# A three-block transformer layer on one core: work by token halves around the latent attention, latents from residual rows, and four-quarter rotary scores

## The chip, the core and the metric

The kernel runs on one core of a Trainium2 chip. TensorE (PE) multiplies matrices into PSUM, VectorE (DVE), ScalarE (ACT) and GpSimd (POOL) work on rows, SyncE (SP) issues nearly all transfers. The metric is the device time in microseconds of one execution. Before the change three runs took 791.65, 786.32 and 791.51 us, median 791.51.

## The reference

There are 256 tokens of 512 values, x, and 4096 context tokens. Three blocks follow each other, each on a layer-normed x, and each is added to x:

```python
x = x + xattn(layernorm(x), ctx, mask, ...)   # 16 heads of 32 over 4096 keys, then an output norm, times gamma, plus beta
x = x + attn(layernorm(x), ...)               # latent attention, causal, 16 heads, below
x = x + ffn(layernorm(x), ...)                # router, top 8 of 48 kept experts, 192 hidden values each
# latent attention
cq = rms_norm(h @ w_qa.T, q_a_ln_w)           # 384 latents; q = cq @ w_qb.T: per head 128 plain + 64 rotary
ckv = h @ w_kva.T                             # 128 latents + 64 rotary key values that all heads share
k_nope, v = split(rms_norm(ckv[..., :128], kv_a_ln_w) @ w_kvb.T)   # per head 128 + 128
pe = pe * cos + rotate_half(pe) * sin         # for queries and for the shared key
out = softmax(causal(q @ k.T * scale)) @ v; return out @ w_o.T
# experts
logits = x @ gate_weight.T; probs = softmax(masked logits); top 8, renormalised
each expert takes its first 192 tokens; y = (silu(x @ g.T) * (x @ u.T)) @ down.T; weighted sum over a token's experts
```

## The kernel before

Everything is written by hand, engine by engine: each engine runs its own list of instructions, and semaphores (`s["..."]`) tie them together. There is no scheduler. Where float16 is used, every operand is split in a high part (a cast on ACT) and a low part (the rest, on DVE), and a product is three matmuls. 256 tokens are two tiles (halves) of 128.

**Cross attention** (to about 336 us) goes over eight context blocks; the change leaves it as it is but for its last output products and one helper, `prep_experts`, that DVE ran in the last block.

**First way around** (L781 to L815 on DVE, L1143 to L1161 on PE). DVE adds the bias to each half's product `d_ps`, takes mean and variance, scales, adds x (this is `x1_sb`), takes mean and variance again and writes the normed rows `xn`. POOL computes each inverse root. PE turns `xn` (transposes), ACT copies the turned rows to `xT`, PE multiplies by `wlatT` to the latents (384 + 128 columns) and to the rotary keys, once as they are and once with their two halves swapped (columns written twice in the weights). Root mean squares, scaling, turning (`lat_ps`), and the split into `lath` and `latl` follow. Then the first pair's projections, in the order q, rotary q (with swapped copies), k, v.

**Eight pairs of heads** (`mla_pair` on each engine). On PE: scores of pair m (plain part, then rotary part, for each half), projections of pair m+1 (q, rotary q plain and swapped, k), output product of pair m-1 for half 0, turning of the probabilities, output product for half 1, the product with v, projection of v. On DVE: causal mask, row maxima, probabilities' scaling, low parts, rotation of the queries (five operations), low part of the output weights, low part of pair m+2's q weights (`split_q`, L699), low part of the result. PE waits for DVE at `p_ready` and for ACT at `pt_ready`.

**Second way around** (L891 on): the sum into `x1_sb`, the norm of both halves, turning, logits, top 8, counts over earlier tokens (`tri`, `ones`), router weights `ex`, turned to `wT`, gathered by the one-hot `emap` to 48 rows `wnew`, stored to memory (`w_scratch`) and loaded back as rows repeated over 64 partitions (`wb`).

**72 expert units** of 128 hidden values. On PE `gate_up(n)` is 24 matmuls of 256 columns, `down(n)` six of 512; the order is gate_up(0), gate_up(1), down(0), gate_up(2), down(1) and so on. ACT takes the silu, DVE multiplies (L930), weighs with `wb` (L933) and splits into `hh`, `hl`. Each unit's weights (768 KB) are loaded and split, ACT `uwh` (L557), DVE `uwl` (L875). The splits of units 0, 1 and 2 stand on DVE before pair 6, before pair 7 and after pair 7.

PE's matmuls all pass through one helper, L962, so its lines don't tell them apart; tiles and shapes do.

## Time and profile before

| | us |
|---|---|
| median of three runs | 791.51 |
| the profiled execution's own time | 791.05 |
| its span, first to last instruction | 789.3 |
| PE busy | 741.8 (94%) |
| DVE busy | 607.5 (77%) |
| ACT busy | 410.9 (52%) |
| mean granted TensorE clock | 0.978 |

In a row of instruction groups stand the line, engine, operation, tiles, shapes and count, then total busy us and the mean ns of one, then the idle time before. In a timeline row the first number is the start in us from the span's start, the second the duration of the row's instructions together; in brackets stands how long the engine had been idle and who released it. A PE row's duration includes the drain of its last matmul, in which the next row has already begun. A stretch row gives the stretch, its length, and for each engine busy us and instructions; then the granted TensorE clock (1.00 is 2.4 GHz, 0.50 is 1.2 GHz), the DMA engines' busy share and GB/s. The chain of waits gives PE 71% of the span, 19% to issue on an engine that waited for nothing shown, 5% to DVE, 2% to ACT.

### The profile page before, as it was taken

The numbers are of one execution on the slowest core, as the hardware profiler recorded it, in microseconds if no ns is written. First come the engines' busy times: TensorE is split into PE (matmuls) and PEld (weight loads), VectorE is DVE, ScalarE is ACT, GpSimd is POOL, SyncE is SP. The second block draws the span as 40 slices with busy tenths as digits, with TensorE's granted clock in tenths as the row PEclk, the third lists the DMA queues.
The fourth block names the chain that finished last, engine by engine and source line by source line (L and its number), as shares of the span: only waits on it lengthen the run. The fifth ranks groups of instructions, "written<-read, shape, count | busy, mean of one in ns | idle before, by whom it ended". The sixth has DMA issues, their size and how long they took to land.

```text
span 789.3 us, 16744 instructions
## 1 busy us (share of the span) xinstructions
PE 741.8 (94%) x6813; PEld 458.9 (58%) x6813; DVE 607.5 (77%) x964; ACT 410.9 (52%) x538; POOL 10.3 (1%) x29
## 2 busy tenths in 40 slices
PE   8999999999999998977999966699999999999997
PEld 3544444444444444435777744477777777777774
DVE  4598888888888887745798855488888888888885
ACT  3666676666667676403567642244444444444441
POOL 2000000000000000010000000000000000000000
PEclk9999999999999999989999987999999999999999
DMA  8910110101000100050242200397777777776760
GB/s 321 336 56 15 42 53 3 56 2 55 2 2 1 55 2 3 1 213 0 81 152 88 105 1 0 107 285 237 235 234 233 233 233 233 233 238 229 238 230 27
DMA packets 30211, 96.09 MB, mean 122 GB/s; under 512 B 6048, under 2 KB 15696, under 8 KB 27728
## 3 DMA queue, kind: packets, MB, share of 16 engines
q1 hardware_dynamic: 29872, 95.33, 36.4%
q8 instruction: 39, 0.64, 0.3%
q14 instruction: 12, 0.10, 0.0%
q10 hardware_dynamic: 288, 0.02, 0.0%
HBM read 94.73 MB, written 0.57 MB: 121 GB/s over the span
## 4 chain that ended last, share of the span: by engine, by line
PE 71%; issue 19%; DVE 5%; ACT 2%; DMA 1%; POOL 0%; POOLq 0%; DVEq 0%; SPq 0%; ACTq 0%
PE pS L962 31%; PE pP L962 24%; PE pD L962 8%; PE pO L962 8%; DVE xT L740 2%; ACT arena L467 2%; DVE arena L629 0%; PE pS L974 0%; DVE bn L776 0%; DMA arena<-w_scratch 0%; DMA w_scratch<-arena 0%; DVE xn L623 0%; DVE arena L755 0%; PE pS L1146 0%; DVE x_sb L789 0%
## 5 line engine op out<-in xcount | busy, mean ns | idle before, releaser
L962 PE MATMUL pS<-arena 128*128 128x256 f16 (+1 forms) x2178 | 260.4, 277 | 4.6 <-DVE arena L814 1.9
L962 PEld LDWEIGHTS pS<-arena 128*128 128x128 f16 (+1 forms) x2178 | 217.8, 102 | 51.8 <-issue 6.9
L962 PE MATMUL pP<-arena 128*128 128x512 f16 x968 | 237.1, 384 | 2.5 <-DVE arena L629 2.5
L962 PEld LDWEIGHTS pP<-arena 128*128 128x128 f16 x968 | 91.2, 99 | 127.9 <-issue 24.3
L467 ACT ACTIVATE arena<-pS,mblk 128x1024 f32<-128x1024 f32 x128 | 147.3, 1201 | 14.1 <-PE pS L962 11.5
L875 DVE SCALAR_TENSOR_TENSOR arena<-arena 128x1536 f16<-128x1536 f32 x72 | 126.1, 1752 | 3.0 <-ACT arena L557 3.0
L728 DVE TENSOR_SCALAR arena<-arena 128x1024 f32<-128x1024 f32 x128 | 88.3, 692 | 43.3 <-ACT arena L467 40.0
L574 ACT ACTIVATE arena<-pS 128x256 f32<-128x256 f32 x72 | 27.7, 384 | 164.2 <-PE pS L962 164.2
L557 ACT ACTIVATE arena<-arena 128x1536 f16<-128x1536 f32 x72 | 106.3, 1477 | 0.8 <-DMA arena<-in_units 0.8
L962 PE MATMUL pO<-arena 128*32 128x256 f32 (+6 forms) x1272 | 100.1, 366 | 2.7 <-DVE arena L835 2.7
L962 PE MATMUL pD<-arena 128*128 128x512 f16 x288 | 77.2, 382 | 7.5 <-DVE arena L937 6.0
L962 PEld LDWEIGHTS pO<-arena 128*32 128x32 f32 (+3 forms) x1272 | 43.3, 107 | 38.1 <-issue 18.0
L930 DVE TENSOR_TENSOR arena<-pS,arena 128x256 f32<-128x256 f32 x72 | 30.6, 424 | 38.7 <-ACT arena L574 38.7
L962 PE MATMUL pS<-work,arena 32*128 32x256 f16 x1536 | 53.4, 269 | 3.2 <-ACT arena L467 3.0
L962 PEld LDWEIGHTS pS<-work,arena 32*128 32x128 f16 x1536 | 33.9, 93 | 32.5 <-issue 24.5
L409 ACT ACTIVATE arena<-pP,xb 128x512 f32<-128x512 f32 x29 | 20.0, 688 | 46.2 <-PE pP L962 46.2
L962 PEld LDWEIGHTS pD<-arena 128*128 128x128 f16 x288 | 27.9, 98 | 25.6 <-DVE arena L937 6.7
L933 DVE TENSOR_TENSOR arena<-arena 128x256 f32<-128x256 f32 x72 | 30.7, 426 | 13.1 <-DMA arena<-w_scratch 5.7
L740 DVE TENSOR_TENSOR xT<-xT,arena 128x1024 f32<-128x1024 f32 x28 | 34.2, 1222 | 1.5
L740 DVE TENSOR_TENSOR arena<-arena 128x1024 f32<-128x1024 f32 x28 | 34.2, 1222 | 1.5
L414 ACT ACTIVATE arena<-pP 128x512 f32<-128x512 f32 x29 | 17.3, 597 | 31.6 <-PE pP L962 31.6
L937 DVE TENSOR_TENSOR arena<-arena 128x256 f16<-128x256 f32 x72 | 30.7, 426 | 2.5
(191 smaller groups left out, 505.7 us busy)
## 6 DMA issues: line engine op xcount, KB each, us to landing
arena<-in_units SPq DMA_DIRECT2D x72, 768.0 KB, 4.8
arena<-w_scratch SPq DMA_DIRECT2D x144, 64.0 KB, 2.7
mw_in<-in_mla_in SPq DMA_DIRECT2D x8, 1024.0 KB, 7.7
...
```

The costliest lines, as they stand in the source:

```text
L409: act.activation(kf[:, n % 2], bank, ACT.Identity, bias=xb[:, 1, n:n + 1], scale=1.0 / SW).then_inc(s["proj_evac"], 1)
L414: act.activation(v_sb[:, p, n - HC], bank, ACT.Copy, scale=1.0 / (SA * SW)).then_inc(s["proj_evac"], 1)
L467: act.activation(probs[:, tile], step_scores(st), ACT.Exp, bias=mblk[:, p, 1, tile:tile + 1], scale=mblk[:, p, 0, tile:tile + 1])\
L557: act.activation(uwh[:, slot], uw32[:, slot], ACT.Copy, scale=SW).then_inc(s["unit_hi"], 1)
L574: act.activation(sg[:, buf], pS[:, bank, 0:T], ACT.Silu, scale=1.0 / (SA * SW)).then_inc(s["silu_ready"], 1)
L728: dve.tensor_scalar(probs[:, t], probs[:, t], LO, HI, ALU.max, ALU.min).then_inc(s["clip_done"], 1)
L740: dve.tensor_tensor(acc, acc, probs[:, t], ALU.add).then_inc(s["sum_done"], 1)
L875: dve.scalar_tensor_tensor(uwl[:, slot], uw32[:, slot], SW, uwh[:, slot], ALU.mult, ALU.subtract).then_inc(s["unit_lo"], 1)
L930: dve.tensor_tensor(m1[:, buf], pS[:, bank, T:2 * T], sg[:, buf], ALU.mult).then_inc(s["m1_ready"], 1)
L933: dve.tensor_tensor(m2[:, buf], m1[:, buf], wb[:, slot], ALU.mult).then_inc(s["m2_ready"], 1)
L937: dve.tensor_tensor(hl[:, buf], m2[:, buf], hh[:, buf], ALU.subtract).then_inc(s["h_lo"], 1)
L962: return pe.matmul(o, lhsT, rhs, start=start, stop=stop, **kw)
```

## The change

- **First way around.** The latents come from the turned residual rows `x1_sb` themselves. PE sums the columns of `wlatT` (`col_sums`), and DVE forms mean times column sum minus product (`center`), which is minus the centred latents; the inverse root of the layer norm isn't applied to the latents at all, their root mean square takes it in through a scaled epsilon (`epsv`). Only the rotary keys are scaled by it. Rotary keys are computed as rows (128 columns: plain and swapped), scaled, and turned. The halves go through one after the other; the cross attention's last products too. Twenty warming matmuls are gone. `prep_experts` moves behind the second statistics, and also clears the gate's unwanted columns.
- **Rotary scores.** A query's rotary part is projected once, without a swapped copy. It is multiplied by cosine and by sine (`qcs`, one operation), and the keys have two turned forms, so that the scores take two rotary products instead of one. The weights `mw_in` are 1152 instead of 1536 columns wide for q.
- **Pairs.** v's projection moves ahead of the turning; the first pair's order is k, v, rotary q, q; units 0, 1, 2 are split within pairs 4, 5, 6 (behind the maxima on DVE).
- **Last pair.** `mla_last_pair` goes by halves, with own banks and semaphores.
- **Second way around.** Norm, turning, logits and choice by halves; masking by a matmul of `nkeep` into the logits' bank; softmax's sum over the top 8 alone. The router weights of units 0 to 3 are spread over the partitions by PE itself (`bc_ps`), three units' gate_up stand before the first down, `wnew` is copied by ACT and stored later.
- **Experts.** Three `hh`/`hl` buffers, four `sg`, the first twelve units written out. Units 4 to 7 are loaded ahead, ahead of the store.

```diff
+            for n in range(RING):
+                sp.wait_ge(s["unit_lo"], n + 1)
+                load_unit(n + RING, n)
             sp.wait_ge(s["wn_ready"], 1)
             sp.dma_start(wdram, wnew[0:KEPT, :]).then_inc(s["w_stored"], 16)
             sp.wait_ge(s["w_stored"], 16)
-            for u in range(RING):
+            for u in range(RING, 2 * RING):
...
+                if proj:
+                    rope_hi(m + 1, 1 - p)
...
+                dve.scalar_tensor_tensor(x1_sb[:, t, :], work[:, t, :], rstd[:, t:t + 1], x_sb[:, t, :],
+                                         ALU.mult, ALU.add).then_inc(s["xn_ready"], 1)
+            for t in range(TT):
+                dve.wait_ge(s["xn_ready"], t + 2)
                 half_stats(x1_sb, t)
+                dve.tensor_scalar(epsv[:, t:t + 1], mv[:, t, 1:2], 1e-5, 1e-6, ALU.add, ALU.mult)
                 dve.tensor_scalar(var[:, t:t + 1], mv[:, t, 1:2], 1e-5, None, ALU.add).then_inc(s["var_ready"], 1)
-            for t in range(TT):
+            prep_experts()
...
+                dve.scalar_tensor_tensor(latc[:, t], colsum[:, 0:LAT], mv[:, t, 0:1], pS[:, 2 + t, :],
+                                         ALU.mult, ALU.subtract).then_inc(s["latc_ready"], 1)
...
-                dve.wait_ge(s["lrstd_ready"], t + 1)
-                dve.tensor_scalar(cqn[:, t], pS[:, 2 + t, 0:QLR], lrs[:, t, 0:1], None, ALU.mult)
-                dve.tensor_scalar(kvn[:, t], pS[:, 2 + t, QLR:QLR + KVLR], lrs[:, t, 1:2], None, ALU.mult)\
...
-                dve.scalar_tensor_tensor(rp1, pS[:, 1, 0:T], SH / (SA * SW), cosT[:, :], ALU.mult, ALU.mult).then_inc(s["rope_step"], 1)
-                dve.scalar_tensor_tensor(rp2, pS[:, 1, T:2 * T], SH / (SA * SW), sinT[:, :], ALU.mult, ALU.mult).then_inc(s["rope_step"], 1)
...
-                dve.tensor_tensor(qpel[:, p], rp1, qpeh[:, p], ALU.subtract).then_inc(s["rope_ready"], 1)
...
+            center(0)
+            scale_kpe(0)
+            add_eps(0)
+            norm_latents(0)
+            center(1)
+            scale_kpe(1)
+            add_eps(1)
+            norm_latents(1)
...
+                dve.scalar_tensor_tensor(qcs, pS[:, 1, 0:T].unsqueeze(1).broadcast_to([128, 2, T]), SH / (SA * SW), cs,
+                                         ALU.mult, ALU.mult).then_inc(s["rope_mul"], 1)
...
+                dve.tensor_tensor(qpel[:, p], qcs, qpeh[:, p], ALU.subtract).then_inc(s["rope_ready"], 1)
...
+                dve.scalar_tensor_tensor(qcs, kpeT, SH, cs[:, 0].unsqueeze(1).broadcast_to([128, 2, T]), ALU.mult, ALU.mult)
...
+                if unit is not None:
+                    split_unit(unit, unit)
...
+                    rope_mul(m + 1, 1 - p)
                     lo_q(m + 1, 1 - p)
-                    rope_q(m + 1, 1 - p)
                     lo_k(m + 1, 1 - p)
+                    rope_lo(m + 1, 1 - p)
...
+            rope_k_products()
+            lo_latents()
+            rope_k()
+            lo_k(0, 0, 1)
+            rope_mul(0, 0, 3)
...
+                for t, (lo, hi) in enumerate(((0, 128), (128, 384))):
+                    dve.wait_ge(s["exps_done"], m + 1 + t)
+                    dve.reciprocal(rc[:, t], sm[:, t]).then_inc(s["rec_ready"], 1)
+                    dve.wait_ge(s["rec_ready"], m + 1 + t)
+                    for j in range(2):
+                        last = dve.tensor_scalar(pm[:, j, lo:hi], pm[:, j, lo:hi], rc[:, t, j:j + 1], None, ALU.mult)
+                    last.then_inc(s["p_ready"], 1)
...
+            for t, o in enumerate((pD, pP)):
+                dve.wait_ge(s["mla_done"], t + 1)
+                link(dve.scalar_tensor_tensor(x1_sb[:, t, :], o[:, :], 1.0 / (SH * SW), x1_sb[:, t, :], ALU.mult, ALU.add))
+                half_stats(x1_sb, t)
+                dve.tensor_scalar(var[:, t:t + 1], mv[:, t, 1:2], 1e-5, None, ALU.add).then_inc(s["var_ready"], 1)
...
-            for t in range(TT):
+            for t in range(TT):
+                pe.wait_ge(s["ctxn_ready"], 2)
                 out_rows(t, (2,))
-            for t in range(TT):
                 pe.wait_ge(s["ctxn_ready"], t + 3)
                 out_rows(t, (3,)).then_inc(s["delta_done"], 1)
...
-            keep_warm(20)
-            pe.wait_ge(s["lat_in"], 16)
...
+            def col_sums(o, lo, hi):
+
+                for c in range(HC):
+                    last = mm(o, ones[:, :], wlatT[:, c, lo:hi], c == 0, c == HC - 1)
+                last.then_inc(s["col_mm"], 1)
...
-                    last = pe.transpose(pS[:, t, 128 * c:128 * c + 128], xn[:, t, 128 * c:128 * c + 128], ident[:, :])
+                    last = pe.transpose(pS[:, t, 128 * c:128 * c + 128], x1_sb[:, t, 128 * c:128 * c + 128], ident[:, :])
...
+            def rotary_keys(t):
                 for c in range(HC):
-                    at = QLR + KVLR + 128 * r
-                    last = mm(pO[:, 1, T * r:T * r + T], wlatT[:, c, at:at + 128], xT[:, c, :], c == 0, c == HC - 1)
-            last.then_inc(s["kpe_mm"], 1)
-            for t in range(TT):
+                    last = mm(kpe_ps[t], xT[:, c, 128 * t:128 * t + 128], wlatT[:, c, LAT:], c == 0, c == HC - 1)
...
+            pe.wait_ge(s["lat_in"], 16)
+            col_sums(pD[:, :], 0, LAT)
+            turn_rows(0)
+            pe.wait_ge(s["ctxn_ready"], TT + 2)
+            col_sums(pO[:, 1, 0:2 * DR], LAT, LAT + 2 * DR)
+            turn_rows(1)
+            latents(0)
+            rotary_keys(0)
+            latents(1)
+            rotary_keys(1)
+            pe.wait_ge(s["col_ready"], 2)
+            turn_keys(0)
+            turn_latents(0)
+            turn_keys(1).then_inc(s["kpe_tr"], 1)
+            turn_latents(1).then_inc(s["lat_tr"], 1)
...
-                for r in range(2):
+                for r in ((1, 0) if first else (0, 1)):
...
-                    for j in range(2):
+                    for j in range(2 - r):
...
-                        for j in range(2):
-                            last = mm(pO[:, j, lo:hi], q[64 * j:64 * j + 64, p, 128 * t:128 * t + 128],
-                                      w[64 * j:64 * j + 64, 0:hi - lo], False, k == 2)
-                last.then_inc(s["s_done"], 1)
+                        for i in range(2):
+                            for j in range(2):
+                                r = slice(64 * j, 64 * j + 64)
+                                last = mm(out_of(t, j, lo, hi), q[r, p, i, 128 * t:128 * t + 128], w[r, i, 0:hi - lo],
+                                          start and k == 0 and i == 0, stop and k == 2 and i == 1)
...
+                nope(0, 0, 128, True, False)
+                half = rotary(0, 0, 128, False, True)
+                if apart:
+                    half.then_inc(s["s_done"], 1)
+                    pe.wait_ge(s["qkv_ready"], 3 * m + 3)
+                rotary(1, 128, 384, True, False)
+                nope(1, 128, 384, False, True).then_inc(s["s_done"], 1)
...
                     out_product(m - 1, 1 - p, 0)
+                pe.wait_ge(s["qkv_ready"], 3 * m + 3)
+                if proj:
+                    proj_v()
...
-                pe.wait_ge(s["qkv_ready"], 3 * m + 3)
                 if proj:
-                    pe.wait_ge(s["rope_step"], 4 * m + 6)
+                    pe.wait_ge(s["rope_mul"], m + 2)
...
-                if proj:
-                    proj_v()
...
+            proj_k(0, first=True)
+            proj_v()
             proj_q(0, first=True)
-            pe.wait_ge(s["lat_lo"], QC + 1)
-            proj_k(0)
...
+            def mla_last_pair(m, p):
+
+                def turned(t):
+                    pe.wait_ge(s["p_ready"], m + 1 + t)
+                    for j in range(2):
+                        for i in range(t + 1):
+                            at = 128 * (t + i)
+                            last = pe.transpose(tail_s[t][:, j, 128 * i:128 * i + 128], pm[:, j, at:at + 128], ident[:, :])
+                    last.then_inc(s["pt_done"], 1)
+
+                def weighted(t):
+                    pe.wait_ge(s["pt_ready"], m + 1 + t)
+                    for j in range(2):
+                        for i in range(t + 1):
+                            last = mm(tail_o[t][:, j, :], vv[:, p, i, 128 * j:128 * j + 128],
+                                      pt[:, j, 128 * (t + i):128 * (t + i) + 128], i == 0, i == t)
+                    last.then_inc(s["o_done"], 1)
+
+                mla_scores(m, p, apart=True)
+                out_product(m - 1, 1 - p, 0)
+                turned(0)
+                weighted(0)
+                turned(1)
+                out_product(m - 1, 1 - p, 1)
+                weighted(1)
+                for t in range(TT):
+                    out_product(m, p, t, last=True).then_inc(s["mla_done"], 1)
+
...
+            keep_warm(8, pS[:, 0, :])
...
+                pe.wait_ge(s["xT_ready"], t + 4)
+                mm(pO[:, t, 0:NEXP], ident[:, :], nkeep, True, False)
+                for c in range(HC):
+                    last = mm(pO[:, t, 0:NEXP], xT[:, c, 128 * t:128 * t + 128], gateT[:, c, :], False, c == HC - 1)
+                last.then_inc(s["logits_done"], 1)
...
+            gate_up(1, 1, 1)
             pe.wait_ge(s["w_ready"], 1)
...
-            mm(pS[0:KEPT, 3, 0:T], emap, wT, True, True).then_inc(s["wn_done"], 1)
+            for n in range(RING):
+                e = 2 * (n // 3) + (0 if n % 3 == 2 else n % 3)
+                pick = pick2 if n % 3 == 2 else emap[:, e:e + 1].broadcast_to([128, 128])
+                last = mm(bc_ps[:, n], pick, wT, True, True)
+            last.then_inc(s["bc_done"], 1)
+            mm(wn_ps, emap, wT, True, True).then_inc(s["wn_done"], 1)
+            gate_up(2, 2, 2)
...
+                    if not (last_turn and u + 1 >= UNROLL) and not (first and u < 2):
                         gate_up(n + 1, (u + 1) % 3, (u + 1) % RING)
```

PE in one pair of the loop, before: 24 matmuls of scores, then 42 of projections (`pS`, 128x256).

```order
L962 MATMUL pO<-arena 128x128 x12
L962 MATMUL pO<-arena 128x256 x12
L1170 REGISTER_ALU
L1171 REGISTER_ALU
L1173 REGISTER_ALU
L962 MATMUL pS<-arena 128x256 x42
L962 MATMUL pD<-arena 128x512 x6
L1237 MATMUL pO<-ident,arena 128x128 x6
L962 MATMUL pP<-arena 128x512 x6
```

And with the change:

```order
L1113 MATMUL pO<-arena 128x128 x18
L1113 MATMUL pO<-arena 128x256 x18
L1348 REGISTER_ALU
L1349 REGISTER_ALU
L1351 REGISTER_ALU
L1113 MATMUL pS<-arena 128x256 x33
L1113 MATMUL pD<-arena 128x512 x6
L1435 REGISTER_ALU
L1113 MATMUL pS<-arena 128x256 x6
L1441 MATMUL pO<-ident,arena 128x128 x6
L1113 MATMUL pP<-arena 128x512 x6
```

Scores are 36 matmuls, 12 more, all rotary; the projections ahead of the output product fell from 42 to 33, and the six of v stand before the turning (`pO<-ident`) instead of at the pair's end.

PE from the last pair's scores to the sum of its output products, before:

```order
L962 MATMUL pO<-arena 128x128 x12
L962 MATMUL pO<-arena 128x256 x12
L962 MATMUL pD<-arena 128x512 x6
L1237 MATMUL pO<-ident,arena 128x128 x6
L962 MATMUL pP<-arena 128x512 x6
L962 MATMUL pS<-arena 128x256
L962 MATMUL pS<-arena 128x128
L962 MATMUL pS<-arena 128x256
L962 MATMUL pS<-arena 128x128
L962 MATMUL pD<-arena 128x512 x6
L962 MATMUL pP<-arena 128x512 x6
L962 MATMUL pD<-zero 128x512
```

And with the change:

```order
L1113 MATMUL pO<-arena 128x128 x18
L1113 MATMUL pS<-arena 128x256 x18
L1113 MATMUL pD<-arena 128x512 x6
L1469 MATMUL pO<-ident,arena 128x128 x2
L1113 MATMUL pS<-arena 128x128 x2
L1469 MATMUL pS<-ident,arena 128x128 x4
L1113 MATMUL pP<-arena 128x512 x6
L1113 MATMUL pS<-arena 128x128 x4
L1113 MATMUL pD<-arena 128x512 x6
L1113 MATMUL pP<-arena 128x512 x6
L1113 MATMUL pS<-zero 128x512 x8
```

The last pair's turning (`<-ident`) and its v products (`pS`, 128x128) are two halves, the second half's turning ahead of pair 6's second output product. The closing zero product (`pD<-zero`) is gone, and eight warming ones (`pS<-zero`) stand at the end.

PE around the router weights, from the counts to the first down products, before:

```order
L962 MATMUL pO<-arena,tri 128x128
L962 MATMUL pO<-arena,ones 128x128
L962 MATMUL pO<-arena,tri 128x128
L1308 MATMUL pS<-ident,arena 128x128 x2
L962 MATMUL pS<-arena 48x256
L1320 UNCONDITIONAL_BRANCH
L1320 ISA
L962 MATMUL pS<-arena 128x256 x24
L1291 REGISTER_ALU
L962 MATMUL pD<-arena 128x512 x3
L962 MATMUL pP<-arena 128x512 x3
```

And with the change:

```order
L1113 MATMUL pS<-arena,tri 128x128
L1113 MATMUL pS<-arena,ones 128x128
L1113 MATMUL pS<-arena,tri 128x128
L1113 MATMUL pS<-arena 128x256 x24
L1541 MATMUL pS<-ident,arena 128x128 x2
L1113 MATMUL pO<-arena 128x256 x4
L1113 MATMUL pS<-arena 48x256
L1113 MATMUL pS<-arena 128x256 x24
L1113 MATMUL pD<-arena 128x512 x3
L1113 MATMUL pP<-arena 128x512 x3
L1113 MATMUL pD<-arena 128x512 x3
L1113 MATMUL pP<-arena 128x512 x3
```

Four products with a picked column (`pO<-arena 128x256 x4`) are new, and three gate_ups (x24) stand before the first down (pD, pP) instead of two.

## Rows read from the trace of the kernel before

**Rows 1.** Stages: engines' busy us, granted TensorE clock, DMA.

```profile
0.00:335.90 335.90, 327.29 (x3759) 155.37 (x3760) 267.24 (x367) 216.44 (x245) 4.86 (x22) 1.00 0.17 59
335.90:373.80 37.90, 27.64 (x120) 16.41 (x119) 19.25 (x43) 7.91 (x19) 4.73 (x6) 0.86 0.28 111
373.80:477.00 103.20, 93.57 (x738) 68.66 (x738) 79.69 (x161) 59.60 (x124) 0.00 (x0) 0.95 0.23 82
477.00:504.90 27.90, 14.24 (x84) 11.33 (x84) 13.53 (x40) 6.54 (x12) 0.69 (x1) 0.81 0.05 14
504.90:785.00 280.10, 279.02 (x2114) 207.18 (x2114) 226.52 (x354) 120.43 (x138) 0.00 (x0) 0.99 0.70 224
```

**Rows 2.** Short stretches of TensorE alone: busy us, instructions, granted clock.

```profile
344.40:351.20 6.80, 5.80 (x10) 0.50 0.50 208
...
363.50:371.20 7.70, 7.55 (x50) 0.78 0.00 0
...
463.80:470.80 7.00, 3.72 (x12) 0.51 0.00 0
```

**Rows 3.** Instruction groups, 373 to 460 us: busy, mean ns, idle before.

```profile
L699 DVE SCALAR_TENSOR_TENSOR arena<-mw_in,arena 128x1536 f16<-128x1536 f32 x7 | 12.3, 1753 | 0.2 <-ACT arena L442 0.2
...
L830 DVE SCALAR_TENSOR_TENSOR arena<-pS,arena 128x512 f16<-128x512 f32 x7 | 4.8, 684 | 0.0
...
L529 ACT ACTIVATE arena<-pS 128x512 f16<-128x512 f32 x7 | 4.2, 597 | 4.4 <-PE pS L962 4.4
```

**Rows 4.** Timeline between the two attentions: start, us, instruction, idle before.

```profile
344.72 1.09 PE L1146 MATMUL pS<-ident,xn 128*128 128x128 f32 x4 [4.30 <-DVE xn L795]
...
346.49 6.02 PE L962 MATMUL pS<-wlatT,xT 128*128 128x512 f32 x8 [0.69 <-ACT xT L496]
...
353.64 3.70 PE L962 MATMUL pS<-wlatT,xT 128*128 128x512 f32 x8 [0.69 <-ACT xT L496]
...
361.70 0.84 ACT L550 ACTIVATE arena<-pS,lnw 128x256 f16<-128x256 f32 x2 [3.49 <-PE pD L1161]
...
373.79 2.38 PE L962 MATMUL pO<-arena 128*128 128x128 f16 x24 [2.67 <-DVE arena L835]
```

**Rows 5.** Timeline of one pair, and the next pair's start.

```profile
386.42 0.50 PE L962 MATMUL pO<-arena 128*128 128x128 f16 x6
...
387.88 0.50 PE L962 MATMUL pO<-arena 64*128 64x256 f16 x6
...
388.32 4.76 PE L962 MATMUL pS<-arena 128*128 128x256 f16 x42
...
392.45 1.01 DVE L859 TENSOR_SCALAR arena<-arena 128x128 f32<-128x128 f32 x4
...
398.17 1.97 PE L962 MATMUL pO<-arena 128*128 128x128 f16 x24
```

**Rows 6.** Timeline: pair 6's scores, then the last pair.

```profile
445.14 1.97 PE L962 MATMUL pO<-arena 128*128 128x128 f16 x24
...
458.12 1.97 PE L962 MATMUL pO<-arena 128*128 128x128 f16 x24
...
460.32 1.76 DVE L875 SCALAR_TENSOR_TENSOR arena<-arena 128x1536 f16<-128x1536 f32 x1 [1.34 <-ACT arena L557]
...
467.08 1.54 PE L1237 MATMUL pO<-ident,arena 128*128 128x128 f32 x6 [5.59 <-DVE arena L859]
```

**Rows 7.** Timeline, attention's sum to the first down product.

```profile
477.02 0.69 DVE L891 SCALAR_TENSOR_TENSOR x_sb<-pD,x_sb 128x512 f32<-128x512 f32 x1 [0.93 <-PE pP L962]
...
482.39 1.97 PE L974 MATMUL pS<-ident,xn 128*128 128x128 f32 x8 [5.41 <-DVE xn L623]
...
497.69 0.36 SPq L310 DMA_DIRECT2D w_scratch<-arena  x1
...
504.93 1.46 PE L962 MATMUL pD<-arena 128*128 128x512 f16 x3 [5.00 <-DVE arena L937]
```

**Rows 8.** Ten expert units, all engines.

```profile
512.00:551.15 39.15, 39.15 (x303) 29.34 (x301) 32.38 (x51) 17.69 (x21) 0.00 (x0) 1.00 0.80 257
```

487 lines of the change are left out of this document (296 added, 191 removed).

## The prediction

> **What bounds the kernel now.** I read the stages first [rows 1]. TensorE (PE) is busy 327.3 of 335.9 us in cross attention and 279.0 of 280.1 us in the expert units: both are full, and the change touches neither's inside. Between them stand 37.9 us of which PE works 27.6, partly at a low clock (0.86), 103.2 us of pairs of heads (93.6 busy, 0.95) and 27.9 us of which 14.2 are busy (0.81). What can be won lies in these 169 us. In the expert units ten take 39.15 us, 3.915 each, PE 100% busy, DVE 32.4 [rows 8]: work that is done before the first down product is no longer due behind it. Next the single waits. PE waits 4.30 us for the normed rows, 2.67 for the first pair's low parts [rows 4], 5.59 for the last pair's probabilities [rows 6], 5.41 for the normed rows of the second way around and 5.00 for the router weights' round trip through memory [rows 7]. Last the clock: after a stretch in which PE did little it is granted 0.50 (1.2 GHz): 344.4 to 351.2, about half of 363.5 to 371.2, 463.8 to 470.8 [rows 2]. The latents' first half took 6.02 us so, the second half 3.70 [rows 4].
>
> Prices [rows 3]: DVE 0.68 us for 512 columns, 1.75 for 1536 (in proportion between); ACT 0.60 for 512. A float32 product of 512 columns is 0.43 per MATMUL row (eight rows in 3.70 with a drain of about 0.3). A float16 one of 256 columns is 0.11 (42 in 4.76) [rows 5].
>
> **First way around.** Marks are those of the profiled execution. Half 0's bias sum can start 0.85 us sooner, because its last product no longer stands behind half 1's (two MATMUL rows of 0.43). PE turned `xn` at 344.72; it now turns `x1_sb`, written before the second statistics: those, the power on POOL and the scaling fall out, some 4.3 us, so PE turns half 0 at about 339.6. The column sums (3.4 and 0.9 us) run while PE would wait, in place of warming products, so they cost nothing and keep the clock up; if their cover went they would cost 4.3. Half 1 is turned at 341.1. Then PE is continuous: latents 3.4, keys 0.9, latents 3.4, keys 0.9, from 341.6 to 350.1. `prep_experts` (about 2.3 us of DVE) ends near 345.8, and half 0's latents are ready at 345.2: 0.6 late, hidden since DVE then waits for half 1. Half 1's latents are there at 349.5; centring 0.7, keys 0.8, squares on ACT 1.0, epsilon and power 1.0, scaling 0.6 end at 353.2, turning at 353.8, against 361.70: 7.9 us won. From there the scores came 12.1 us later. Now DVE is the chain: the keys' two products 1.3 (from 353.2), low parts of the latents 1.6, keys' sums and split 2.0, k 0.7, the query's rotation 0.7, its cast on ACT 0.7 and low part 0.7, q 0.7: 361.7. PE has 39 products (4.3 us at full clock) instead of 48 and is hidden behind this, unless it runs at 1.2 GHz: it idles most of 350 to 354, and then q's evacuation comes after 362.7 and the scores at 364. I take 363.3 for 373.79: **10.5 us won** (8 to 12).
>
> **Pairs 0 to 6.** A pair takes 11.75 us (386.42 to 398.17) and PE is never idle in it [rows 5]. q's projections lose nine products of 256: 9 x 0.11 = 0.98. The scores gain twelve rotary products. Do these cost what others cost? Six rotary ones of 256 columns start at 387.88 and the next block at 388.32 [rows 5]: 0.44 for six, where one behind another they take 0.66. So the two heads' products, on rows 0 to 63 and 64 to 127, run as pairs, and 0.44 is three pairs of 0.11 and about 0.1 of changing over. Added are three narrow and three wide pairs, 0.17 + 0.33 = 0.5. By the Trainium skill (TensorEngine Tiling (Array Packing), Key Properties) a change of the tiling mode drains TensorE; the trace agrees with its 0.1 per change. Both halves' rotary blocks now stand side by side, two changes instead of four: 0.2 less. Net 0.98 - 0.5 + 0.2 = 0.68 less, 11.1 a pair. v's projection is moved, not added. DVE follows if its chain is shorter: it was idle 0.2 us before a pair's mask, so 11.55; five rotary operations (1.9) become two of 512 (1.3), the low part of q's weights goes from 1536 to 1152 columns (-0.4): 10.5. The probabilities are scaled at 393.46, 5.1 us after the scores (388.4) [rows 5]; PE's wait for them stays covered: 33 products, the output product and v make 3.6 + 1.3 + 0.65 = 5.55. ACT's new cast (0.6) stands before its copy of the turned probabilities, which then ends at about 7.45 where PE asks at 7.5: covered by nothing to spare; without cover it costs 0.6 a pair. Pair 0, without output products, is a chain and not full: 11.4 instead of 12.6. Pairs 1 to 3 win 0.65 each. In pairs 4 to 6 a unit's split (1.75) fills DVE's 1.2 us wait for the exponentials and delays the probabilities by 0.55, PE by 0.3: they take 11.4, against 11.75 twice and 12.98 (445.14 to 458.12 [rows 6], with a split before the mask). Sum 1.2 + 2.0 + 0.7 + 1.6 = **5.5 won** (-1 to 6.5).
>
> **Last pair.** Scores began at 458.12 and the sum on DVE at 477.02 [rows 6, 7]: 18.9 us, with a split of 1.76 before the mask, 5.59 of waiting and 7 us at low clock after it. By halves, counted from the scores' start: v's evacuation holds half 1's scores to 1.55, they end at 3.0, output product 4.3; DVE has half 0's probabilities at 5.25 and half 1's at 6.4; ACT, behind its copy of the output weights (1.05), turns them over at 7.1; v for half 0 to 7.5, turning 8.0, pair 6's second output product 9.3, v for half 1 10.2, output product of half 0 11.5, seen by DVE at 11.7. PE is still idle some 2.5 us from 4.3 to 7.1, so I add 1.2 for low clock: 12.9, **6.0 won** (3.5 to 7.2).
>
> **Second way around and start of the units.** From that mark (0) the first down came at 27.9, with two gate_ups done, and 1.7 us more went to low clock behind it (the stage from 504.9 has 0.99). Now half 0 is normed at 4.3, half 1 at 5.2 (5.4 for both before); turning and copies 7.35, logits 6.9 and 7.9, low parts 8.9, gate_up(0) from 9.0 to 11.6, counts 12.3, gate_up(1) 14.9 (router weights ready at 13.2, hidden), turning and copy 15.8, four spreading products 17.6, `wnew` 18.0, gate_up(2) 20.6, down(0) and down(1) 23.2, then a wait for unit 3's split: ACT's silu and cast, DVE's unit 2 and 1.75, to 24.9. At 24.9 three gate_ups and two downs are done, 3 x 2.62 + 2 x 1.30 = 10.5 us of work, against 5.2 at 27.9: 3.0 + 5.2 = 8.3, and 1.7 of clock, less 1.5 for low clock in the new order (two waits of 1 to 1.5 us near 3 to 5): **8.5 won** (5 to 10). The store of the router weights waits in SP's queue behind unit 7's load, until 24.9; from the store (497.69) to the first use (504.93) were 7.2 us with 1.3 of DVE's work [rows 7], so they are there at 31, where unit 4 asks at 32. If late, PE waits as long as they are, 1 or 2 us.
>
> **Sum.** 10.5 + 5.5 + 6.0 + 8.5 = 30.5. Of hand-written hand-overs priced to 0.1 us some fail; I take off 1.5. 791.05 - 29 = 762.0 in the profile's frame; the median stands 0.46 higher: **762.5 us**.
>
> **Rivals.**
> - *The clock eats it.* By the Trainium skill (TensorE: Matmul & The Clock Gate, What's actually happening) low clock is the default that sustained activity lifts. Work by halves gives PE small pieces with gaps. From the rows: each low stretch costs half of PE's work in it, 1.7 to 3.4 us. Against: most gaps are shorter than before. With three more such stretches, 770. Chance 0.13.
> - *The pairs stay where they were.* If rotary products didn't pair, 12 x 0.11 or 0.06 make 1.0 for 0.98 saved; or ACT's cast before the copy holds PE 0.6 a pair. Then pairs win 1 instead of 5.5, and the last pair, with the same ACT queue, 2 less: 769. For: ACT's slack of nothing. Chance 0.12.
> - *Halves give back.* The added small operations lengthen both ways around, and each wins only half: 778. Chance 0.04.
> - *The change doesn't do what it says*, the latents' chain still waiting for statistics through `epsv`: DVE does them by 343.4, before the latents exist. Costs at most 5: 767. Chance 0.02.
> - *Slower:* the units' loads become the pace. SP now waits for unit 3's split before the store; DMA is 80% busy already [rows 8]. If the queue never caught up and each unit came late, 72 units would have to lose over 0.53 us each (beyond 4.45 a unit) to pay back 30 us and 8 more: 800. Against: in steady state the same bytes in the same order. Chance 0.01.
>
> Forecast's own case 0.68. Range 753 to 773: below by the better ends of two stages and the half percent by which runs differ (786.32 to 791.65), above to the first two rivals. One percent, 8 us, is about what runs can tell from no change: faster 0.96, same 0.03, slower 0.01.
>
> **What would show it.** Turning of half 0 right behind the column sums, with no clock loss before 350; the first pair's scores near 363; 11.1 us from pair to pair, PE without a wait; 36 score products in 2.2 us; the last pair under 13 us to DVE's sum; first down about 21 us later, three gate_ups done; then 3.915 a unit. Wrong if PE waits for ACT's copy in every pair, if the units' period moves, or if low clock shows inside the pairs.

## The result

The changed kernel takes 756.38 us, median of four runs (755.16 to 757.53), the kernel before beside it 791.42 (786.32 to 791.65): ratio 0.9579, 95% interval 0.9549 to 0.9609. Forecast were 762.5 us and 753 to 773. The profiled execution took 755.26 us with a span of 753.4, 35.8 us less than the one profiled before; the sum forecast 29.

The stages of the changed kernel, columns as in [rows 1], cut at the same events: the end of cross attention, the first pair's scores, VectorE's sum behind attention, and the first down product (the last row is ten units).

```profile
0.00:336.70 336.70, 327.41 (x3759) 155.42 (x3760) 266.46 (x363) 216.23 (x245) 4.88 (x22) 1.00 0.17 57
336.70:362.10 25.40, 21.18 (x110) 13.06 (x108) 20.83 (x54) 8.66 (x21) 4.10 (x6) 1.00 0.40 158
362.10:451.20 89.10, 84.70 (x768) 64.46 (x769) 74.56 (x145) 60.96 (x135) 0.00 (x0) 1.00 0.31 110
451.20:471.80 20.60, 18.44 (x135) 13.96 (x134) 12.37 (x37) 6.04 (x14) 1.35 (x2) 1.00 0.00 1
471.80:749.10 277.30, 274.92 (x2092) 204.20 (x2089) 225.16 (x350) 121.86 (x139) 0.00 (x0) 1.00 0.69 217
500.00:539.15 39.15, 39.15 (x303) 29.35 (x301) 32.38 (x51) 17.58 (x21) 0.00 (x0) 1.00 0.75 238
```

To read: the three middle stages lasted 37.9, 103.2 and 27.9 us in [rows 1] and last 25.4, 89.1 and 20.6 now. The clock stands at 1.00 everywhere (0.86, 0.95, 0.81 before). Ten units still take 39.15 us with VectorE at 32.38, as in [rows 8].

The timeline of TensorE (and, at 354.52, ScalarE) through the first way around; it answers to [rows 4].

```profile
336.75 3.60 PE L1113 MATMUL pD<-wlatT,ones 128*128 128x512 f32 x8
340.42 0.66 PE L1300 MATMUL pS<-ident,x_sb 128*128 128x128 f32 x4
...
342.36 8.82 PE L1113 MATMUL pS<-wlatT,xT 128*128 128x512 f32 x32
...
353.83 0.33 PE L1317 MATMUL pD<-ident,arena 128*128 128x128 f32 x1 [1.19 <-DVE arena L883]
...
354.52 0.47 ACT L582 ACTIVATE arena<-pO,lnw 128x256 f16<-128x256 f32 x1 [2.44 <-PE pO L1317]
...
355.14 4.72 PE L1113 MATMUL pS<-arena 128*128 128x256 f16 x39 [0.66 <-ACT arena L582]
...
362.15 2.36 PE L1113 MATMUL pO<-arena 128*128 128x128 f16 x36 [1.85 <-DVE arena L931]
```

Half 0 is turned right behind the column sums; the products of both halves' latents and rotary keys, 32 rows, run without a gap and at full speed (8.82 us, where the latents of half 0 alone took 6.02 in [rows 4]).

The score blocks of pairs 1, 2, 5, 6 and the last (the pairs are counted from 0); then TensorE's waits in the last pair and behind it.

```profile
373.01 2.37 PE L1113 MATMUL pO<-arena 128*128 128x128 f16 x36
...
384.04 2.37 PE L1113 MATMUL pO<-arena 128*128 128x128 f16 x36
...
417.34 2.37 PE L1113 MATMUL pO<-arena 128*128 128x128 f16 x36
...
428.59 2.37 PE L1113 MATMUL pO<-arena 128*128 128x128 f16 x36
...
439.85 0.94 PE L1113 MATMUL pO<-arena 128*128 128x128 f16 x18
441.19 1.60 PE L1113 MATMUL pS<-arena 64*128 64x256 f16 x18 [0.40 <-ACT arena L577]
...
444.83 0.44 PE L1469 MATMUL pO<-ident,arena 128*128 128x128 f32 x2 [0.74 <-DVE arena L1009]
...
446.52 0.71 PE L1113 MATMUL pS<-arena 128*128 128x128 f32 x4 [1.25 <-ACT arena L609]
...
451.19 0.69 DVE L1025 SCALAR_TENSOR_TENSOR x_sb<-pD,x_sb 128x512 f32<-128x512 f32 x1 [0.46 <-PE pD L1113]
...
455.25 0.66 PE L1497 MATMUL pS<-ident,xn 128*128 128x128 f32 x4 [1.08 <-DVE xn L1030]
...
471.76 0.81 PE L1113 MATMUL pD<-arena 128*128 128x512 f16 x3
...
475.84 2.79 PE L1113 MATMUL pS<-arena 128*128 128x256 f16 x24 [1.33 <-DVE arena L941]
```

Pair to pair are 11.03 us, 11.25 where a unit's split stands in the pair, against 11.75 [rows 5]. The wait of 5.59 us in the last pair [rows 6] has become 0.40, 0.74 and 1.25. The wait of 5.41 for the normed rows [rows 7] has become 1.08 behind eight warming products (452.29 to 454.18), so TensorE is without useful work for 2.8 us there, against 5.8. In place of the wait of 5.00 for the router weights stands none ahead of the first down product, and 1.33 ahead of the fourth gate_up. The program's first part is 0.67 us later in this execution, already at 301 us, ahead of all that the change touches.

### The profile page after: what moved, and what is told of

Same layout as the page of the kernel before. It is cut to its first block, busy times and chain, and to the rows that moved or that the text cites. A ratio compares the mean times of both kernels' runs of the same rounds, so it can differ in the third digit from the quotient of the medians.

```text
span 753.4 us, 16700 instructions
## 1 busy us (share of the span) xinstructions
PE 726.6 (96%) x6859; PEld 451.1 (60%) x6859; DVE 600.6 (80%) x948; ACT 413.7 (55%) x553; POOL 10.3 (1%) x30
## 4 chain that ended last, share of the span: by engine, by line
PE 85%; DVE 6%; issue 4%; ACT 3%; POOL 1%; POOLq 0%; DVEq 0%; ACTq 0%
PE pS L1113 38%; PE pP L1113 26%; PE pO L1113 10%; PE pD L1113 9%; DVE xT L806 2%; ACT arena L485 2%; PE pO L1441 1%; DVE arena L691 0%; DVE bn L842 0%; DVE arena L821 0%; DVE arena L941 0%; DVE arena L893 0%; DVE xn L685 0%; ACT arena L535 0%; DVE work L847 0%
## 5 line engine op out<-in xcount | busy, mean ns | idle before, releaser
L1113 PE MATMUL pS<-arena 128*128 128x256 f16 (+2 forms) x2128 | 251.5, 274 | 5.1 <-DVE arena L941 1.3
L1113 PEld LDWEIGHTS pS<-arena 128*128 128x128 f16 (+2 forms) x2128 | 210.9, 101 | 49.5 <-ACT arena L552 2.2
L1113 PE MATMUL pO<-arena 128*32 128x256 f32 (+6 forms) x1358 | 103.4, 358 | 2.4 <-DVE arena L931 1.9
L1113 PEld LDWEIGHTS pO<-arena 128*32 128x32 f32 (+3 forms) x1358 | 47.2, 106 | 37.4 <-issue 14.3
L1081 DVE TENSOR_TENSOR arena<-arena 128x256 f32<-128x256 f32 x68 | 29.0, 426 | 7.4 <-DMA arena<-w_scratch 0.5
```

The source lines that it names most:

```text
L1081: dve.tensor_tensor(m2[:, buf], m1[:, buf], weight, ALU.mult).then_inc(s["m2_ready"], 1)
L1113: return pe.matmul(o, lhsT, rhs, start=start, stop=stop, **kw)
```

## The experiments

Twelve runs, named by the labels b1, r1 to r6 and a0 to a3 (b1 is an edit of the kernel before, all others of the changed one). Times are medians; the kernel before beside them took 790.33, 790.64 and 789.09 us in the three groups.

**How much is clock alone (b1).** The kernel before, with warming products in TensorE's waits (one of the nine places, of which the first lengthens the old warming from 20 products to 38):

```
                 if before:
                     out_product(m - 1, 1 - p, 0)
+                if not proj:
+                    keep_warm(24, pS[:, 0, :])
```

> The kernel before, with warming products (zero by zero, 0.21 us each) put where TensorE waits: 18 more ahead of the latents, 8 and 11 ahead of pair 0, 24 in the last pair, 24 ahead of the second turning, 28 more in the router's part. None should end after the wait that it fills. It says how much of the gain is clock alone. Theory A: the stretches at 1.2 GHz cost 2.3 us (latents' first half, 6.02 against 3.70), up to 1.7 (pair 0's projections), 1 to 1.5 (last pair) and some 3 to 4 (logits, gate_up, first units): 6 to 9 us, so 783 to 785; the other 27 us of the change are shorter paths. Theory B (the clock is the gain): 20 us or more, below 772. Theory C (warming products delay what they stand before): no gain, 790 or more.

Measured: 781.77 us (781.39 to 782.64), ratio 0.9907 (0.9872 to 0.9941), mean clock 0.999. By the medians 8.6 us are gained, within the 6 to 9 of theory A. This profile is the yardstick for the rest: the same program at full clock. Its marks of the same four events (scores of pair 0 and of the last pair, VectorE's sum, the last zero product):

```profile
369.83 1.96 PE L962 MATMUL pO<-arena 128*128 128x128 f16 x24 [0.29 <-issue]
...
452.62 1.97 PE L962 MATMUL pO<-arena 128*128 128x128 f16 x24
...
469.78 0.69 DVE L891 SCALAR_TENSOR_TENSOR x_sb<-pD,x_sb 128x512 f32<-128x512 f32 x1 [0.93 <-PE pP L962]
...
775.32 0.38 PE L962 MATMUL pP<-zero 128*128 128x512 f16 x1
```

With before's 373.79, 458.12, 477.02 and 784.53, and the changed kernel's 362.15, 439.85, 451.19 and 748.62, every stage splits in two. "Clock" is before less warmed, "shorter path" is warmed less changed:

| stage | before | before, warmed | changed | clock | shorter path |
|---|---|---|---|---|---|
| start to pair 0's scores | 373.79 | 369.83 | 362.15 | 4.0 | 7.7 |
| pairs 0 to 6 | 84.33 | 82.79 | 77.70 | 1.5 | 5.1 |
| last pair | 18.90 | 17.16 | 11.34 | 1.7 | 5.8 |
| second way and units | 307.51 | 305.54 | 297.43 | 2.0 | 8.1 |
| sum | | | | 9.2 | 26.7 |

The first row holds the executions' different starts too (the warmed one is 0.49 us later than before, the changed one 0.67): without them it is 4.5 and 7.9. The split is that of one profiled execution each; the kernel before also had executions of 786 to 789 us at a mean clock of 0.982 to 0.985, which lost less to the clock.

**First way around: residual rows (r1).** The wait for the second statistics given back:

```
                 pe.wait_ge(s["xn_ready"], t + 2)
+                pe.wait_ge(s["rstd_ready"], t + 2 + TT)
```

> The changed kernel with one wait given back: TensorE turns a half's residual rows only when the rstd of their second statistics is there (POOL's power ends at 343.5 and 344.6 in the changed kernel's profile), as the kernel before had to. Theory A, the path through TensorE's latents sets the first way around: turning of half 0 moves from 340.4 to 343.5, the latents from 342.36 to about 345.1, and the first pair's scores by the same 2.7 us, to 364.9. Total +2.7 us over the changed kernel (756.4), so 759.1, if the clock stays up. Theory B, VectorE's queue sets it (prep_experts and the centring stand there): under +1 us. Theory C, the clock: TensorE then idles 3 us before the latents, which fall to 1.2 GHz and take up to 3 us more: +5 to +6 us, 762.

Measured: 761.71 us (760.82 to 762.73), +5.3 over the changed kernel's 756.38, as all differences from here to r5 are (a0 below, the same kernel again, took 757.53, so they hold to about 1 us). TensorE's timeline of this kernel:

```profile
344.01 1.08 PE L1301 MATMUL pS<-ident,x_sb 128*128 128x128 f32 x4 [3.31 <-POOL rstd L396]
344.88 1.91 PE L1113 MATMUL pO<-wlatT,ones 128*128 128x128 f32 x8
...
359.90 6.38 PE L1113 MATMUL pS<-arena 128*128 128x256 f16 x39 [0.66 <-ACT arena L582]
...
367.74 2.37 PE L1113 MATMUL pO<-arena 128*128 128x128 f16 x36 [1.03 <-DVE arena L931]
```

The wait delays the turning by 3.2 us (theory A), and B falls. The clock comes on top, but not where C had it: the latents still take 8.82 us. Directly behind the wait the turning and the short column sum take 1.08 and 1.91 instead of 0.66 and 1.06, which costs 1.2. The projections take 6.38 instead of 4.72, which costs 0.8 ahead of the scores. That fall can't be put down to the wait: the kernels of the next section and a1, where no wait was lengthened, show the same (6.01 to 6.39). Another 1.6 us goes to low clock in pairs 0 and 1, as in r3 below.

**Pairs: do two heads' rotary products overlap (r2, r2b)?** First the order alone:

```
-                    for k, (q, w) in enumerate(...):
-                        for i in range(2):
-                            for j in range(2):
+                    for j in range(2):
+                        for k, (q, w) in enumerate(...):
+                            for i in range(2):
```

> The changed kernel with the rotary products of a pair in another order: head 0's six behind one another, then head 1's, instead of the two heads' in turn. Same instructions, same sums. Theory A (the two heads' products on rows 0 to 63 and 64 to 127 run beside each other only when they are issued in turn): 24 products of 0.055 and 0.11 us instead of 12 such times, +1.0 us in each of 8 pairs, a little less in the first and last: +6.5 to +8 us, 764, and 12.1 us from pair to pair instead of 11.1. Theory B (they do not run beside each other, or the order is no matter): the score block keeps its 2.2 us and the total 756.

Measured: 757.68 us (757.43 to 761.28), +1.3, 11.26 us from pair to pair instead of 11.03. A's size a pair was wrong by four times. So a second kernel took the overlap away altogether (`r = slice(0, 64)` for both heads; head 1 then gets head 0's rotary part, so its result is another, with the same products in number and shape):

> The changed kernel, but both heads' rotary products read rows 0 to 63 (this changes what is computed: head 1 gets head 0's rotary part). The order of issue is that of the changed kernel. The run before, with the order changed only, kept most of the overlap: the score block went from 2.37 to 2.60 us. Theory A (what runs beside each other are different row groups, whatever the order): on one row group 24 products cost 12 x 0.055 + 12 x 0.11 = 2.0 us instead of 1.0, the score block 3.3 to 3.5 us, +1.0 us in 7 pairs and in the last: +7 to +9 us, 764. Theory B (narrow products are simply cheaper than 0.055 and 0.11, with no overlap of rows): no change, 756 to 758.

Measured: 764.32 us (763.72 to 765.39), +7.9, 12.01 us a pair. The groups of the twelve wide and the twelve narrow rotary products of one pair (x12; busy us, mean ns), for the changed kernel, head after head, and one row group:

```profile
L1113 PE MATMUL pO<-arena 64*128 64x256 f16 x12 | 0.8, 268 | 0.0
...
L1113 PE MATMUL pO<-arena 64*128 64x128 f16 x12 | 0.5, 217 | 0.0
```

```profile
L1113 PE MATMUL pO<-arena 64*128 64x256 f16 x12 | 1.1, 270 | 0.0
...
L1113 PE MATMUL pO<-arena 64*128 64x128 f16 x12 | 0.6, 217 | 0.0
```

```profile
L1113 PE MATMUL pO<-arena 64*128 64x256 f16 x12 | 1.5, 268 | 0.0
...
L1113 PE MATMUL pO<-arena 64*128 64x128 f16 x12 | 0.8, 215 | 0.0
```

Each product takes as long as ever (about 268 and 217 ns); what changes is how many run at once. Products on different row groups overlap, and most of the overlap stays when the heads are issued one after the other: that order loses 0.23 us a pair, one row group 0.98. By the Trainium skill (TensorEngine Tiling (Array Packing), Key Properties) different tiles can execute matmuls in parallel; the trace agrees, with those 0.98 us.

How the overlap survives the order, two views of 0.02 to 0.03 us of the kernel with the heads one after the other show. They list what is running then, and each gives the start of the earliest product:

```profile
385.82 0.51 PE L1113 MATMUL pO<-arena 64*128 64x256 f16 x5
...
385.90 0.43 PE L1113 MATMUL pO<-arena 64*128 64x128 f16 x4
```

All twelve narrow products are issued ahead of the first wide one, yet head 0's first wide product starts at 385.82 and a narrow one of head 1 only at 385.90. So each row group works through its own products, and one runs ahead of the other; starts are in the order of issue only within a row group.

**Pairs: v's projection moved (r6).** Back behind the product with v:

```
-                pe.wait_ge(s["qkv_ready"], 3 * m + 3)
-                if proj:
-                    proj_v()
                 pe.wait_ge(s["p_ready"], m + 1)
...
                 pe.wait_ge(s["pt_ready"], m + 1)
+                pe.wait_ge(s["qkv_ready"], 3 * m + 3)
...
                 last.then_inc(s["o_done"], 1)
+                if proj:
+                    proj_v()
```

> The changed kernel with v's projection back behind the product with v, at a pair's end. Theory A (v's projection covers the wait for the probabilities, which are ready 0.26 us after the output product, and for ScalarE's copy of the turned ones): +0.2 to +0.5 us in each of 7 pairs, +1.5 to +3 us, 758.5, with a TensorE wait on VectorE or ScalarE in every pair. Theory B: no wait appears, within 0.5 us of 756.

Measured: 764.06 us (762.96 to 764.59), +7.7. Theory A's waits are there, at more than its price of 1.5 to 3. Pair 2 to pair 3 of this kernel:

```profile
386.79 2.37 PE L1113 MATMUL pO<-arena 128*128 128x128 f16 x36
...
394.28 0.88 PE L1438 MATMUL pO<-ident,arena 128*128 128x128 f32 x6 [0.23 <-DVE arena L967]
...
398.47 0.71 PE L1113 MATMUL pO<-arena 128*128 128x128 f16 x10
```

11.68 us a pair: 0.07 less than before's 11.75 [rows 5]. The shorter projections and the fewer changes of tiling win nothing while TensorE waits for VectorE and then for ScalarE's copy; moving v is what turns the shorter work into time. Of the extra 0.65 a pair, 0.39 lie ahead of the turning: it starts 1.68 us behind the start of the output product, which takes 1.29 elsewhere (the row counts 0.23 of this as idle, the rest as drain). ScalarE's copy, which ends at 396.18, holds the product with v another 0.13 us, to 396.43; the remainder is spread over two small gaps.

In pairs 4 to 6, where a unit's split stands, the loss is 0.82 each. So pairs 1 to 6 lose 4.4 us, and pair 0 the 0.65 of v's projection, which no longer fills a wait there: 5.1 us of path. The other 2.7 of this execution are low clock behind pair 0's turning (1.5) and in the last pair (1.2).

**Where units 0 to 2 are split (r4).** Ahead of pair 6, ahead of and behind the last pair, as before:

```
             for n in range(3):
-                mla_pair(PAIRS - 4 + n, n % 2, ahead=n < 2, unit=n)
+                if n == 2:
+                    split_unit(0, 0)
+                mla_pair(PAIRS - 4 + n, n % 2, ahead=n < 2)
+            split_unit(1, 1)
             mla_last_pair(PAIRS - 1, 1)
+            split_unit(2, 2)
```

(ScalarE's halves of the splits move likewise.)

> The changed kernel with the first three units' splits where the kernel before has them: ahead of pair 6, ahead of the last pair, behind the last pair, instead of in VectorE's wait for the exponentials of pairs 4 to 6. Theory A (a split ahead of a mask, or ahead of the residual sum, stands on the path): pair 6 +1.2 us, as before (12.98 against 11.75), the last pair +1.6, the third split 1.48 + 1.75 us on ScalarE and VectorE behind the last low part, of which 0.5 is covered, +2.5: together +5 us, 761.5, pairs 4 and 5 unchanged at 11.1. Theory B (placement is no matter, the engines have slack): within 1 us of 756.

Measured: 766.76 us (763.5 to 768.9), +10.4, twice theory A's size. Its TensorE timeline: pair 0's scores, pair 6's wait, the last pair's scores, its wait for the probabilities, pair 6's second output product, and the turning behind attention:

```profile
362.11 3.16 PE L1122 MATMUL pO<-arena 128*128 128x128 f16 x36 [1.85 <-DVE arena L936]
...
436.10 0.83 PE L1122 MATMUL pS<-arena 128*128 128x256 f16 x6 [1.71 <-DVE arena L776]
...
441.99 0.94 PE L1122 MATMUL pO<-arena 128*128 128x128 f16 x18
...
449.34 0.69 PE L1478 MATMUL pO<-ident,arena 128*128 128x128 f32 x2 [3.12 <-DVE arena L1014]
...
452.90 2.77 PE L1122 MATMUL pP<-arena 128*128 128x512 f16 x6
...
464.12 0.66 PE L1506 MATMUL pS<-ident,xn 128*128 128x128 f32 x4 [3.23 <-DVE xn L1039]
```

Three waits of 1.71, 3.12 and 3.23 us where the changed kernel has none, 0.74 and 1.08. From the last pair's scores to that turning are 22.1 us instead of 15.4: the 4.5 us of longer waits, and low clock between them (2.77 us for products that take 1.46).

The profiled execution (765.4) is 10.1 us longer than the changed kernel's. Of these, 5.5 are the path: 1.2 up to the last pair's scores and 4.3 from there to the turning, about what theory A priced (5). Low clock behind the longer waits is 3.6. The last 1.0 is low clock in pair 0 (the first row: 3.16 us instead of 2.36, behind the same wait of 1.85), ahead of everything that this edit moves. By the medians no other single edit cost more; by the best executions r6 is its equal (763.5 and 762.96). In pairs 4 and 5, now without a split, the period is 11.02 instead of 11.25, so a split in the wait for the exponentials costs 0.23 us.

**The last pair by halves (r3).** Worked whole, like the others (on ScalarE and VectorE too):

```
-            mla_last_pair(PAIRS - 1, 1)
+            mla_pair(PAIRS - 1, 1, proj=False)
+            for t in range(TT):
+                out_product(PAIRS - 1, 1, t, last=True).then_inc(s["mla_done"], 1)
```

> The changed kernel with its last pair worked whole, as all other pairs, instead of by token halves. Theory A (the halves shorten the chain at the end): pair 0 of the changed kernel, which has no output products either, shows the chain: 9.5 us from the scores to the products with v, then 1.4, 0.6, 0.7 and 2.6 for output products: 14.9 to VectorE's sum, less some 0.9 for a split that this pair lacks, against 11.34: +2.5 to +4 us, 759.5. If TensorE's idle time before the turning (over 3 us) takes the clock down, +1 to +2 more. Theory B (the chain of small operations by halves gives back what it wins): within 1 us of 756.

Measured: 761.46 us (759.69 to 762.1), +5.1. Scores at 441.92, VectorE's sum at 457.63: 15.7 us against 11.34, with a wait of 3.92 and low clock behind it; the first row is pair 0's:

```profile
372.08 2.93 PE L1113 MATMUL pS<-arena 128*128 128x256 f32 x8 [1.09 <-ACT arena L552]
...
449.50 0.85 PE L1441 MATMUL pO<-ident,arena 128*128 128x128 f32 x6 [3.92 <-DVE arena L967]
450.18 2.48 PE L1113 MATMUL pP<-arena 128*128 128x512 f16 x6
452.45 2.18 PE L1113 MATMUL pS<-arena 128*128 128x256 f32 x8
```

Of these 4.4 us, 1.7 are low clock: the six output products take 1.0 us more and the next eight 0.7 more than in other pairs. The path is 2.7, and theory A, with the clock that it allowed for, holds. This execution's last product comes 6.4 us later than the changed kernel's; the rest of that is a later start (0.5) and low clock behind pair 0's turning (2.93 us instead of 1.58, behind the same wait), 1.6 in all, ahead of the edited part.

**Router weights of the first units through memory (r5)**, three gate_ups ahead as in the changed kernel. Besides what is shown, SyncE loads units 4 to 7 behind the store again and not ahead of it, so the run takes back both:

```
-                if isinstance(n, int) and n < RING:
-                    dve.wait_ge(s["bc_done"], 1)
-                    weight = bc_ps[:, n]
-                else: ...
+                dve.wait_ge(wb_in[slot], 32 * (loads + 1))
+                weight = wb[:, slot]
```

> The changed kernel with the router weights of the first four units read back from memory, as for all later ones, instead of spread by four TensorE products; three gate_ups still run ahead. Theory A: wnew is there 2 us sooner (four products fewer), stored at about 467.6; store to first down product took 7.2 us in the kernel before, so 474.9 against 471.8: +3 to +3.5 us, 759.7; the clock may fall in a wait of 5 us, +1. Theory B (three gate_ups ahead cover the round trip): within 1 us of 756. Theory C (the loads behind the store come late for units 4 and 5): over +5 us, with waits on DMA in the first ten units.

Measured: 761.12 us (759.7 to 762.07), +4.7. TensorE's first down product:

```profile
477.10 1.46 PE L1105 MATMUL pD<-arena 128*128 128x512 f16 x3 [4.19 <-DVE arena L1077]
```

From turning to the first down 477.10 - 458.17 = 18.9 us instead of 16.5, +2.4, with a wait of 4.19. Behind it the first units run at low clock (1.46 us for three products that take 0.81), another 1.5. The other 2.9 us of the profiled execution (762.07) lie ahead of the edited part: 0.3 of later start, and low clock in pair 0 (3.21 us instead of 2.36 for the scores) and in the last pair, with their waits unchanged. The best execution, 759.70, had a mean clock of 0.997 and fits theory A. B falls; so does C, for no unit behind the first waits for a load.

**Two waits that are left, and the clock.** The changed kernel again, and three edits of it on one chip:

> The changed kernel again, unedited, beside the three below. Four executions so far gave 755.2 twice (mean clock 1.00) and 757.5 twice (0.995). Expected: 756.4, and both values again.

> The changed kernel with two waits taken out. In the last pair ScalarE's copy of the output weights (1.05 us) goes ahead of the exponentials, into its idle 1.27 us, so TensorE's 1.25 us wait for the turned probabilities goes. Unit 3 is split while TensorE runs gate_up(1) (ScalarE behind the router's exponentials, VectorE behind the router weights), so the 1.33 us wait ahead of gate_up(3) goes. Theory A (both waits are on the path): -2 to -2.6 us against the changed kernel beside it, the first scores to TensorE's end 386.9 minus that. Theory B (the next wait takes over: VectorE's split delays the copy of wT, or the exponentials come later): 0 to -1 us.

> The changed kernel with 14 small warming products in TensorE's waits between the turned latents (0.37 and 1.19 us: 2 and 8 of 256 columns, 0.11 each) and ahead of pair 0's scores (1.85 us: 4 of 512, 0.21 each). In several profiles of edited kernels the stretch behind these waits ran at 1.2 GHz, with all engines before it at the same marks as in the changed kernel. Theory A (these gaps decide whether the clock falls): no execution at 757.5 any more, all near 755.2, clock 1.00. Theory B (chance, or another place): spread from 755 to 757.5 as without. Theory C: warming delays the turning or the scores, +0.3 to +1.

> Both edits of a1 and both of a3. Theory A: they add up, -2 to -2.6 for the waits and the median of the lucky executions for the clock: 753, all executions within 0.5 us of each other, mean clock 1.00. Theory B: warming costs what it gives, 754 and as a1.

```
             def mla_last_pair(m, p):            # ScalarE; the copy leaves its old place
+                act.wait_ge(mout_in[p], 16 * (m // 2 + 1))
+                act.activation(woh[:, p], mw_out[:, p], ACT.Copy, scale=SW).then_inc(s["wo_hi"], 1)
...
             last.then_inc(s["w_ready"], 1)      # VectorE; ScalarE behind ex_ready
+            split_unit(3, 3)
...
+            keep_warm(8, pP[:, 256:512])        # a2 and a3 only; also 2 and 4
```

| kernel | median | from to | ratio to before |
|---|---|---|---|
| a0, changed | 757.53 | 755.5 to 757.92 | 0.9592 (0.9561 to 0.9622) |
| a1, both waits | 754.20 | 752.73 to 754.48 | 0.9545 (0.9515 to 0.9575) |
| a2, waits and warming | 753.14 | 752.82 to 755.0 | 0.9544 (0.9514 to 0.9575) |
| a3, warming | 757.24 | 755.57 to 757.68 | 0.9585 (0.9555 to 0.9614) |

a1 is 3.3 us faster by the medians, 2.8 by the best executions, both above theory A's 2 to 2.6. The intervals of its ratio and a0's overlap, but all five executions of a1 lie below all five of a0. Free of the clock the gain is 2.3 us: from pair 0's scores to the last zero product a0 takes 386.47 us and a2, with the same two edits and a clock of 0.999, 384.20. So theory A holds, and the rest of the 3.3 is the clock's draw. In a2's profile, at full clock as a0's, the last pair's wait is 0.47 instead of 1.25 and gate_up(3) follows the down products without a wait:

```profile
446.12 0.71 PE L1116 MATMUL pS<-arena 128*128 128x128 f32 x4 [0.47 <-ACT arena L609]
...
473.95 2.78 PE L1116 MATMUL pS<-arena 128*128 128x256 f16 x24
```

Warming alone misses its aim: theory B of a3. In a3's profile it fills the early waits (1.19 and 1.85 us became 0.31 and 0.99) and the projections run at full speed, but the clock falls in the last pair instead: four products with v take 1.23 us, not 0.71.

```profile
355.41 4.72 PE L1113 MATMUL pS<-arena 128*128 128x256 f16 x39 [0.66 <-ACT arena L582]
...
446.79 1.23 PE L1113 MATMUL pS<-arena 128*128 128x128 f32 x4 [1.25 <-ACT arena L609]
```

a2 is the fastest kernel of this study by the median, a1 equal to it within the measurement. Four of a2's five executions lie within 0.4 us (752.82 to 753.22, clock 0.999 to 1.0), the fifth is 755.0; whether warming does more once the last pair's wait is short, five executions don't decide.

## Why the prediction was right, and where it was short

Direction, stages and mechanisms held; the sum was 6.9 us short in the profile's frame (29 against 35.9, the four terms below), each term a little.

- **First way around:** 10.5 forecast, 11.6 measured with a start 0.67 us late, so 12.3. Marks forecast at 339.6, 353.8 and 363.3 came at 340.4, 353.8 and 362.15. The chain after the latents was as worked out; the allowance behind it was not used. That is just above the stage's range of 8 to 12. The waiting that was forecast to fall out is there when it is put back (r1: 3.2 us, and 1.2 of low clock behind it). That the column sums cost nothing the timeline shows: they end when the residual rows of half 0 are written (340.35 and 340.36). That they keep the clock up was not tested, for no run leaves them out.
- **Pairs 0 to 6:** 5.5 forecast, 6.6 measured. 11.03 against 11.1 a pair, 11.25 against 11.4 with a split (the split costs 0.23, not 0.3), pair 0 10.9 against 11.4. The prediction counted v's projection, "moved, not added", among what covers the wait for the probabilities (5.55 us against 5.1), which is right, but it never said what its old place would cost: r6 shows 0.65 a pair, nearly the stage's whole gain of 0.72. That this is near the 0.6 given for an uncovered copy is chance, for the copy's share is 0.13. The copy itself had more room than the "nothing to spare" of the working: it ended at 393.46, and TensorE came for its result at 393.75. The overlap was priced rightly, and for the right reason, two row groups (r2b: 0.98 a pair). VectorE's idle time before a pair's mask was read too small, 0.2 us; in the trace of before it is 0.36, with 0.21 ahead of the low part of q's weights. Nothing came of it.
- **Last pair:** 6.0 forecast, 7.6 measured: 11.34 us against 12.9. The halves come to 11.7 in the working, 0.4 too many; the 1.2 for low clock did not come.
- **Second way and units:** 8.5 forecast, 10.1 measured. The first down came 20.6 us behind the sum, forecast 20.6; units 0 and 1 were down and unit 3 split at 24.65, forecast 24.9. The 1.5 for low clock did not come. The store went out at 476.18, 25.0 us behind the sum as worked out, and TensorE never waited for it.
- **Sum:** the 1.5 taken off for failed hand-overs was not needed.

So the terms that were mis-sized are the allowances: 1.2, 1.5 and 1.5 make 4.2 of the 6.9 us. They were taken because each low stretch in the trace followed a stretch of little work; in the profiled execution all of the new, shorter waits left the clock alone. That is luck in part: five of the nine executions of this kernel took 757.5 to 757.9 us at a mean clock of 0.995, and in those some 2.3 us of the allowances were needed. The rival "the clock eats it" was not idle either: right behind the wait that each of them lengthened, low clock took 1.2 us in r1, 1.7 in r3 and 3.6 in r4. The rival of pairs that stay where they were had two conditions. r2b builds the first, products that don't pair (764.32); r6 comes to the same price by another wait, mostly VectorE's (764.06). The rivals of halves that give back and of loads that set the pace were not met; ten units took 39.15 us before and after.

Not tried: the projections without swapped columns by themselves, the first way with whole rows, and on the second way the norm, the logits and the choice by halves, the masking by a matmul, and the third gate_up ahead. How the 12.3 us of the first way divide beyond what r1 gives back, and the second way's 10.1 beyond the 2.4 of r5, rests on the timelines alone.
